# Decoder layer on one core: the q2c part of the last product folded into its weights

## The chip, the cores and the metric

The kernel runs on one core of a Trainium2 chip, in one launch. The metric is the device time in microseconds (us): a median of 748.32 us over three runs (746.5 to 749.77). Engines are named TensorE (PE), VectorE (DVE), ScalarE (ACT), GpSimd (POOL) and SyncE (SP), which issues all DMAs.

## The reference, cut to what matters

The layer has three parts, each added to its input: self-attention on the normalised x (32 x 112 tokens, width 256), a bidirectional attention with a context (32 x 375 tokens), and a mixture of experts. The change lies in the second. With `c` the normalised x (112 x 256) and `q` the context of one batch element:

```
s       = (c @ w_c + b_c)[:, :, None] + (q @ w_q + b_q)[:, None, :] + einsum('bcd,bqd,d->bcq', c, q, w_cq) + b_cq
c2q_att = softmax(s, axis=2) @ q
b_att   = softmax(max(s, axis=2), axis=1)
q2c_att = einsum('bc,bcd->bd', b_att, c)[:, None, :]        # one row of 256 for each batch element
x       = concatenate([c, c2q_att, c * c2q_att, c * q2c_att], axis=-1)
z       = x @ W_l.T + b_l
```

So z is a sum of four products with the four parts W1 to W4 of the 1024 x 256 weights.

## The kernel before, in words

**Stages.** The first stage runs the attention parts over 8 groups of G = 4 batch elements: group 0, a hardware loop over groups 1 to 6, and group 7. It ends at about 433 us of the profile. The second stage, the experts, follows behind a barrier and is the same in both kernels.

**Products.** Products with weights are made in single pass fp32r from operands split in a high and a low part: `mm3` issues three matmuls (lines 75, 76 and 77) for each block of 128 rows. A product of c, c2q or c * c2q with its part of the weights is thus 2 x 3 = 6 matmuls of 112 x 256 for each element, and z takes 24 for each element. Transposes (`turn_...`), the similarity and c2q products are plain fp32.

**Order.** Every engine has its own instruction list, written out by hand in `group(i, last)`, and waits on semaphores. On TensorE a group is: `qk_product`, `scores`, `v_product` (on h), then `z_q2c(i - 1, 0)` and `(i - 1, 1)`, the c * q2c products of the group before; `probs_proj` and `attention_out`; the last two `z_q2c`; then `turn_c`, `z_c`, `similarity`, `turn_a`, `c2q_product` mixed over the four elements; then `turn_x`, `z_c2q`, `z_x3`, with the next group's `turn_h_pair` between them.

**The q2c path.** VectorE ends a group by `x4` = c * q2c (line 1092). ScalarE takes its high part in the next group between the `qk_copy`s (`x4_high`, line 609, named x_hi in the rows), GpSimd its low part (`x4_low`, line 818, x_lo).

**The other paths into a group.** GpSimd: `x4_low(i - 1)`; `residual_bias(i)`, four additions (line 814); the rstd of each element (lines 830 and 832); `ln1_scalars(i + 1)`; and last x2b = x1 + b_l, four additions (line 844), whose first waits for the store of the group before, since they share the x2b buffer. SyncE: the load of x for the group after next (line 320, behind hh and `residual` of the group), the four context pairs, each behind its `c2q_mm` (lines 303 and 304), and then the store of x2 (line 328). All go through one queue. VectorE starts a group by the statistics of the x just loaded (`ln1_stats`, line 863), three of them ahead of the first `score_max` (line 902).

**The c path.** `c_parts(j)` on ScalarE (lines 657 to 661) copies the transposed c, takes its high part, and scales it by w_cq for the similarity; `c_low(j)` on VectorE (line 949) takes the low part. `residual(i + 1)` on ScalarE (line 604) stands ahead of `c2q_copy(0)` (line 674).

Of the kernel before, what the change touches and what calls it, by code (L numbers as in the profile page):

```python
# [30 lines left out]
P = 128  # L31
# [19 lines left out]
def decoder_layer(nc, x, ctx, ctx_t, norm_w, norm_b, qkv_wt, qk_b, v_b, proj_wt, proj_b, w_cq, b_cq, w_c, b_c,  # L51
# [28 lines left out]
    with outer:  # L80
# [102 lines left out]
        with ExitStack() as c1:  # L183
# [50 lines left out]
            x4_hi, x4_lo = sb("x4_hi", [P, G, KB, L], F32R), sb("x4_lo", [P, G, KB, L], F32R)  # L234
# [12 lines left out]
            x4 = ctw  # L247
# [32 lines left out]
            q2c_ok, x4_ok, x4_hi_ok, x4_lo_ok = sem("q2c_ready"), sem("x4_ready"), sem("x4_hi_ready"), sem("x4_lo_ready")  # L280
# [78 lines left out]
            def _(pe):  # L359
# [30 lines left out]
                def z_q2c(g, j):  # L390
                    if j == 0:
                        pe.wait_ge(x4_lo_ok, g + 1)
                    for k in range(KB):
                        last = mm3(pe, z_of(j), x4_hi[:, j, k, :], x4_lo[:, j, k, :], wl_hi[:, 3 * KB + k, :],
                                   wl_lo[:, 3 * KB + k, :], False, k == KB - 1, skip_group_check=True)
                    if j % 2:
                        last.then_inc(z_mm, 1)

                def group(i, last_group):
# [58 lines left out]
                    def z_c(j):  # L458
                        pe.wait_ge(c_lo_ok, ev[j])
                        if j % 2 == 0:  # L460
                            pe.wait_ge(x2_ok, PAIRS * i + j // 2 + 1)
                        if j == 0 and is_first(i):
                            pe.wait_ge(wl_lo_ok, 1)
                        for k in range(KB):
                            mm3(pe, z_of(j), c_hi[:, j, k, :], c_lo[:, j, k, :], wl_hi[:, k, :], wl_lo[:, k, :],
                                k == 0 and j % 2 == 0, False, skip_group_check=True)

                    def similarity(j):
                        pe.wait_ge(cx_in[j], 32 * (i + 1))
                        pe.wait_ge(ctw_ok, ev[j])  # L470
                        pe.wait_ge(c_lo_ok, ev[j])
# [24 lines left out]
                    def z_c2q(j):  # L496
                        pe.wait_ge(x_lo_ok, ev[j])
                        for k in range(KB):
                            t = slice(k * L, (k + 1) * L)
                            mm3(pe, z_of(j), op_hi[j][:, t], op_lo[j][:, t], wl_hi[:, KB + k, :], wl_lo[:, KB + k, :], False, False,  # L500
                                skip_group_check=True)
# [1047 lines left out]
```

## Time and profile before

| what | value |
|---|---|
| runs | 748.32 us median, 746.5 to 749.77 |
| the profiled execution's own time | 747.58 us |
| its span | 745.8 us |
| TensorE matmul busy | 697.2 us (93%), 4072 instructions |
| VectorE, ScalarE, GpSimd busy | 449.7, 358.0, 199.3 us |
| mean granted TensorE clock | 0.983 |
| DMA | 64.43 MB, mean 86 GB/s |

A matmul's busy time includes its pipelined end, so a busy TensorE is not one at its peak: the distance from start to start is what a matmul costs in a row of them. Idle time of an engine counts only where another engine, or the end, waits for what it does next. Where a loop of waits runs over several engines and a transfer, its length is the period of the groups, and the engine with the most busy time need not be the one that sets it.

### The profile page before, as it was taken

The page shows a single profiled execution, that of the slowest core. Times are in us where ns is not written, and L with a number is a line of the kernel's source. Part 1 is how long each engine was busy: PE and PEld are TensorE (multiplying, and loading weights), DVE is VectorE, ACT ScalarE, POOL GpSimd, SP SyncE. Part 2 cuts the span into 40 slices and gives each one's busy share as a digit, 9 for nine tenths or more (in the row PEclk, how much of TensorE's full clock was granted, in tenths as well). Part 3 has the DMA queues.
Part 4 walks back from the last instruction along what each step waited for, and adds up shares of the span by engine and source line. Part 5 has one row for each costly group of instructions (what it writes and reads, how often), then busy time and mean ns, then how long its engine had stood idle before and what let it go on. Part 6 is the DMA issues. An engine that isn't in the chain of part 4 may idle for free. (4 is left out here: it accounts for less than half of the span.)

```text
span 745.8 us, 12056 instructions
## 1 busy us (share of the span) xinstructions
PE 697.2 (93%) x4072; PEld 588.4 (79%) x4072; DVE 449.7 (60%) x1174; ACT 358.0 (48%) x859; POOL 199.3 (27%) x290
## 2 busy tenths in 40 slices
PE   3999999999999999999999866999999999999997
PEld 2867878778788788788787754788888888888886
DVE  5575655755654646557556665766666667666432
ACT  3755663665656556646665323434242333333331
POOL 2142221314204305223141302232223222232222
PEclk9999999999999999999999887999999999999999
DMA  7505024033051060240420266022222212131200
GB/s 210 155 22 165 6 76 141 0 111 103 0 163 51 22 186 6 77 137 0 123 66 1 75 203 218 1 113 85 115 85 113 86 41 107 50 121 50 114 29 29
DMA packets 50765, 64.43 MB, mean 86 GB/s; under 512 B 3800, under 2 KB 49416, under 8 KB 49840
## 3 DMA queue, kind: packets, MB, share of 16 engines
q1 hardware_dynamic: 50736, 64.06, 27.3%
q8 instruction: 16, 0.26, 0.1%
q14 instruction: 13, 0.11, 0.0%
HBM read 56.60 MB, written 7.45 MB: 86 GB/s over the span
## 5 line engine op out<-in xcount | busy, mean ns | idle before, releaser
L1381 POOL TENSOR_TENSOR sg<-sg,cw_wide 128x512 f32<-128x512 f32 x56 | 73.9, 1319 | 186.6 <-ACT sg L1338 177.0
L1342 ACT ACTIVATE a_hi<-af 128x512 fp32r<-128x512 f32 x63 | 39.8, 632 | 155.8 <-DVE af L1462 155.8
L75 PE MATMUL bank<-h_hi,w_lo 128*128 128x512 f32 x224 | 92.4, 412 | 6.5 <-DVE w_lo L1479 4.7
L76 PE MATMUL bank<-h_lo,w_hi 128*128 128x512 f32 x224 | 90.0, 402 | 0.0
L77 PE MATMUL bank<-h_hi,w_hi 128*128 128x512 f32 x224 | 89.6, 400 | 0.0
L1462 DVE TENSOR_TENSOR af<-bank,sg 128x512 f32<-128x512 f32 x63 | 43.2, 686 | 62.0 <-POOL sg L1381 58.9
L1467 DVE TENSOR_TENSOR a_lo<-af,a_hi 128x512 fp32r<-128x512 f32 x63 | 48.1, 763 | 34.9 <-ACT a_hi L1342 34.9
L75 PE MATMUL bank<-w_hi,a_lo 128*128 128x256 f32 x224 | 63.2, 282 | 0.0
L76 PE MATMUL bank<-w_lo,a_hi 128*128 128x256 f32 x224 | 63.2, 282 | 0.0
L77 PE MATMUL bank<-w_hi,a_hi 128*128 128x256 f32 x224 | 63.1, 282 | 0.0
L844 POOL TENSOR_TENSOR x2b<-x,bl_wide 112x256 f32<-112x256 f32 x32 | 23.1, 753 | 146.6 <-DMA x_scratch<-x2b 146.6
L75 PEld LDWEIGHTS bank<-h_hi,w_lo 128*128 128x128 f32 x224 | 43.6, 195 | 17.3 <-DVE w_lo L1479 5.1
L77 PEld LDWEIGHTS bank<-h_hi,w_hi 128*128 128x128 f32 x224 | 43.2, 193 | 10.2
L76 PEld LDWEIGHTS bank<-h_lo,w_hi 128*128 128x128 f32 x224 | 43.6, 195 | 7.9
L486 PE MATMUL bank<-ctxf,at 125*112 125x256 f32 x192 | 46.7, 379 | 0.0
L473 PE MATMUL bank<-ctxtf,ctw 128*112 128x375 f32 x128 | 46.1, 482 | 0.0
L75 PEld LDWEIGHTS bank<-w_hi,a_lo 128*128 128x128 f32 x224 | 42.5, 190 | 2.5 <-DVE a_lo L1467 0.2
L76 PEld LDWEIGHTS bank<-w_lo,a_hi 128*128 128x128 f32 x224 | 42.5, 190 | 2.3
L1338 ACT ACTIVATE sg<-bank 128x512 f32<-128x512 f32 x63 | 37.1, 589 | 12.3 <-PE bank L77 12.1
L77 PEld LDWEIGHTS bank<-w_hi,a_hi 128*128 128x128 f32 x224 | 42.6, 190 | 0.0
L626 ACT ACTIVATE qg<-bank 112x512 f32<-112x512 f32 x32 | 19.1, 598 | 44.7 <-PE bank L410 44.7
L75 PE MATMUL bank<-wp_hi,op_lo 128*128 128x256 f32 x128 | 39.6, 309 | 0.6 <-DVE wp_lo L990 0.6
(226 smaller groups left out, 1901.0 us busy)
## 6 DMA issues: line engine op xcount, KB each, us to landing
cw_wide<-cw_scratch SPq DMA_DIRECT2D x7, 2048.0 KB, 7.1
ctxtf<-in_ctx_t SPq DMA_DIRECT2D x32, 375.0 KB
ctxf<-in_ctx SPq DMA_DIRECT2D x32, 375.0 KB
xt<-in_x SPq DMA_DIRECT2D x8, 448.0 KB, 8.1
x_scratch<-x2b SPq DMA_DIRECT2D x8, 448.0 KB, 10.7
x2n<-x_scratch SPq DMA_DIRECT2D x7, 512.0 KB, 4.8
x2t<-x_scratch SPq DMA_DIRECT2D x7, 512.0 KB, 4.1
out_dram<-x2t SPq DMA_DIRECT2D x7, 512.0 KB, 2.9
```

Of the source, the lines that this page charges most:

```text
L75: pe.matmul(dst, a_lo, b_hi, start=first, stop=False, **kw)
L76: pe.matmul(dst, a_hi, b_lo, start=False, stop=False, **kw)
L77: return pe.matmul(dst, a_hi, b_hi, start=False, stop=last, **kw)
L473: last = pe.matmul(bank[j][0:L, 0:S], ctw[:, j, k, :], ctxtf[:, j, k, :], start=(k == 0), stop=(k == KB - 1))
L486: last = pe.matmul(bank[j][0:L, 0:D], at[:, j, b * L:(b + 1) * L], ctxf[0:SB, j, b, :], start=(b == 0), stop=(b == NSB - 1))
L626: act.activation(qg[j][0:L, :], bank[j][0:L, :], ACT.Copy).then_inc(qk_ok, 1)
L844: pool.tensor_tensor(x2b[:, j, :], x1[:, j, :], bl_wide[:, :], ALU.add).then_inc(x1b_ok, 1)
L1338: act.activation(sg[b][:, :], g_bank[b][:, :], ACT.Silu).then_inc(sg_ok, 1)
L1342: act.activation(a_hi[n % (AHEAD + 1)][:, :], af[(p + n) % 2][:, :], ACT.Copy).then_inc(a_hi_ok, 1)
L1381: pool.tensor_tensor(sg[b][:, :], sg[b][:, :], cw_wide[p][:, ORDER[n], :], ALU.mult).then_inc(sgw_ok, 1)
L1462: dve.tensor_tensor(af[b][:, :], u_bank[b][:, :], sg[b][:, :], ALU.mult).then_inc(af_ok, 1)
L1467: dve.tensor_tensor(a_lo[b][:, :], af[(p + n) % 2][:, :], f32(a_hi[b][:, :]), ALU.subtract).then_inc(a_lo_ok, 1)
```

## The change

The product of c * q2c with W4 equals c times W4 with its rows scaled by q2c. So for each element of a group VectorE now makes wz = W1 + q2c * W4 (`wz_sum`, two instructions of 128 x 256), ScalarE its high part (`wz_high`), GpSimd its low part (`wz_low`), 128 x 512 each, and TensorE one product with c (`z_c`), in the places of `z_q2c` in the next group. The `z_c` between the transposes of c are gone, and `z_c2q` starts the accumulation. w_cq and w_q are applied on VectorE (`c_weighted`). The high part of c is taken once for the group (`c_high`, 128 x 896, on ScalarE), the low part on GpSimd. `residual(i + 1)` moves on ScalarE behind the c2q copies and `x3_high`, ahead of the last `h_high_pair`.

```
-            wl_f = tmp_all[:, :, :].rearrange("p g (k n) -> p (g k) n", n=D)
+            wl_f = sb("wl_f", [P, 4 * KB, D])
-            wl_hi, wl_lo = sb("wl_hi", [P, 4 * KB, D], F32R), sb("wl_lo", [P, 4 * KB, D], F32R)
+            wl_hi, wl_lo = sb("wl_hi", [P, 2 * KB, D], F32R), sb("wl_lo", [P, 2 * KB, D], F32R)
+            wz = sb("wz", [P, G, KB, D])
+            wz_hi, wz_lo = sb("wz_hi", [P, G, KB, D], F32R), sb("wz_lo", [P, G, KB, D], F32R)
...
# TensorE
-                def z_q2c(g, j):
+                def z_c(g, j):
+                    pe.wait_ge(wz_lo_ok, G * g + j + 1)
                     if j == 0:
-                        pe.wait_ge(x4_lo_ok, g + 1)
+                        pe.wait_ge(c_lo_ok, g + 1)
                     for k in range(KB):
-                        last = mm3(pe, z_of(j), x4_hi[:, j, k, :], x4_lo[:, j, k, :], wl_hi[:, 3 * KB + k, :],
-                                   wl_lo[:, 3 * KB + k, :], False, k == KB - 1, skip_group_check=True)
+                        last = mm3(pe, z_of(j), c_hi[:, j, k, :], c_lo[:, j, k, :], wz_hi[:, j, k, :], wz_lo[:, j, k, :],
+                                   False, k == KB - 1, skip_group_check=True)
...
                     attention_out(3)
-                    z_c(0)
                     turn_c(1)
                     similarity(0)
-                    z_c(1)
                     turn_c(2)
...
# ScalarE
+                def wz_high(g, j):
+                    act.wait_ge(wz_ok, G * g + j + 1)
+                    act.activation(wz_hi[:, j, :, :], wz[:, j, :, :], ACT.Copy).then_inc(wz_hi_ok, 1)
...
                     a_columns(2)
+                    c_high()
                     a_columns(3)
-                    if not last:
-                        residual(i + 1)
                     c2q_copy(0)
...
                     x3_high(3)
...
                     else:
+                        residual(i + 1)
                         h_high_pair(i + 1, 1)
# GpSimd
+                def wz_low(g, j):
+                    pool.wait_ge(wz_hi_ok, G * g + j + 1)
+                    pool.tensor_tensor(wz_lo[:, j, :, :], wz[:, j, :, :], f32(wz_hi[:, j, :, :]), ALU.subtract).then_inc(wz_lo_ok, 1)
...
                 def group(i, last):
-                    if not is_first(i):
-                        x4_low(i - 1)
                     residual_bias(i)
+                    if not is_first(i):
+                        for j in range(G):
+                            wz_low(i - 1, j)
...
                         ln1_scalars(i + 1)
+                    pool.wait_ge(c_hi_ok, i + 1)
+                    pool.tensor_tensor(c_lo[:, :, :, :], ct[:, :, :, :], f32(c_hi[:, :, :, :]), ALU.subtract).then_inc(c_lo_ok, 1)
# VectorE
+                    def c_weighted(j):
+                        dve.wait_ge(ct_ok, ev[j])
+                        for k in range(KB):
+                            w = dve.tensor_scalar(ctw[:, j, k, :], ct[:, j, k, :], wcq[:, k:k + 1], wq[:, k:k + 1], ALU.mult, ALU.add)
+                        w.then_inc(ctw_ok, 1)
+                    def wz_sum(j):
+                        for k in range(KB):
+                            w = dve.scalar_tensor_tensor(wz[:, j, k, :], wl_f[:, 3 * KB + k, :], q2c[:, j, k:k + 1], wl_f[:, k, :], ALU.mult, ALU.add)
+                        w.then_inc(wz_ok, 1)
```

On GpSimd, from the last step of `ln1_scalars` in the loop over groups to the first rstd of the group behind it, before (x2b is x1 with its bias, x4_lo the low part of c * q2c, x2n the residual with its bias, r2a and r2 the rstd):

```order
L809 TENSOR_TENSOR ln1<-ln1,mone 112x4 [waits ln1_scalars]
L843 REGISTER_ALU [waits c_ready]
L844 TENSOR_TENSOR x2b<-x1,bl_wide 112x256 [waits x2_stored]
L844 TENSOR_TENSOR x2b<-x1,bl_wide 112x256 [waits c_ready] x3
L852 REGISTER_ALU
L852 COMPARE_AND_BRANCH
L818 TENSOR_TENSOR x4_lo<-ctw,x4_hi 128x896 [waits x4_hi_ready]
L814 TENSOR_TENSOR x2n<-x2n,pb_wide 112x256 [waits residual_scaled] x4
L830 TENSOR_TENSOR r2a<-mv2,eps 112x1 [waits ln2_moments]
L832 TENSOR_TENSOR r2<-r2a,mhalf 112x1 [waits ln2_var_eps]
```

and in the changed kernel:

```order
L795 TENSOR_TENSOR ln1<-ln1,mone 112x4 [waits ln1_scalars]
L826 TENSOR_TENSOR c_lo<-ct,c_hi 128x896 [waits c_hi_ready]
L832 REGISTER_ALU [waits c_ready]
L833 TENSOR_TENSOR x2b<-x1,bl_wide 112x256 [waits x2_stored]
L833 TENSOR_TENSOR x2b<-x1,bl_wide 112x256 [waits c_ready] x3
L842 REGISTER_ALU
L842 COMPARE_AND_BRANCH
L800 TENSOR_TENSOR x2n<-x2n,pb_wide 112x256 [waits residual_scaled] x4
L804 TENSOR_TENSOR wz_lo<-wz,wz_hi 128x512 [waits c_weights_hi] x4
L817 TENSOR_TENSOR r2a<-mv2,eps 112x1 [waits ln2_moments]
L819 TENSOR_TENSOR r2<-r2a,mhalf 112x1 [waits ln2_var_eps]
```

The low part stood ahead of the four residual additions as one instruction; now it stands behind them as four, one for each element. The low part of c is new, ahead of the x2b additions and their wait for the store.

On TensorE, from the last attention product of a group to the second similarity, before (bank4 holds z of elements 0 and 1; c_lo with wl_hi is the c product):

```order
L449 MATMUL bank3<-qg3,v 112x256
L461 ISA [waits c_lo_ready]
L75 MATMUL bank4<-wl_hi,c_lo 112x256 [waits x2_ready]
L76 MATMUL bank4<-wl_lo,c_hi 112x256
L77 MATMUL bank4<-wl_hi,c_hi 112x256
L75 MATMUL bank4<-wl_hi,c_lo 112x256
L76 MATMUL bank4<-wl_lo,c_hi 112x256
L77 MATMUL bank4<-wl_hi,c_hi 112x256
L455 MATMUL bank1<-ident,c 128x112 [waits c_ready]
L455 MATMUL bank1<-ident,c 128x112
L469 REGISTER_ALU
L473 MATMUL bank0<-ctxtf,ctw 112x375 [waits c_lo_ready,c_weighted,context0_in]
```

and in the changed kernel:

```order
L451 MATMUL bank3<-qg3,v 112x256
L457 MATMUL bank1<-ident,c 128x112 [waits c_ready]
L457 MATMUL bank1<-ident,c 128x112
L464 MATMUL bank0<-ctxtf,ctw 112x375 [waits c_weighted,context0_in]
L464 MATMUL bank0<-ctxtf,ctw 112x375
L457 MATMUL bank2<-ident,c 128x112 [waits c_ready]
L457 MATMUL bank2<-ident,c 128x112
L464 MATMUL bank1<-ctxtf,ctw 112x375 [waits c_weighted,context1_in]
```

The six matmuls for each element that stood among transposes and similarities are gone, and with them the waits for the low part of c; the q2c product, now c with wz, stays where it was.

On ScalarE, behind the copies of the attention columns (at) of a group, before (x2n is the residual, tmp the copied c2q):

```order
L686 ACTIVATE at<-bank2 125x336 [waits a_transposed]
L686 ACTIVATE at<-bank3 125x336 [waits a_transposed]
L604 ACTIVATE x2n<-xt,ln1 112x256 [waits x1_ready,ln1_scalars,x_in]
L674 ACTIVATE tmp<-bank0,sinv2 112x256 [waits sim_inv_sum,c2q_product]
L674 ACTIVATE tmp<-bank1,sinv2 112x256 [waits sim_inv_sum,c2q_product]
L678 ACTIVATE op_hi0<-bank0 128x224 [waits c2q_transposed]
```

and in the changed kernel, at the end of the group:

```order
L665 ACTIVATE op_hi3<-bank3 128x224 [waits c2q_transposed]
L669 ACTIVATE op_hi2<-tmp 128x224 [waits c_c2q_ready]
L669 ACTIVATE op_hi3<-tmp 128x224 [waits c_c2q_ready]
L595 ACTIVATE x2n<-xt,ln1 112x256 [waits x1_ready,ln1_scalars,x_in]
L609 ACTIVATE h3_hi0<-bank7 128x2x224 [waits h_transposed]
```

The residual stood ahead of the c2q copies; now it stands behind the last high part of c * c2q and ahead of the last high part of h.

## Rows read from the trace of the kernel before

**Rows 1.** The longest waits: engine, line, releaser: us in total, times, longest.
```profile
POOL x2b L844 <- DMA x_scratch<-x2b: 146.6, 7, 22.9
...
DVE st L863 <- DMA xt<-in_x: 38.2, 7, 6.9
```

**Rows 2.** SyncE's queue in order of time: start, us, engine, line, transfer issued.
```profile
156.12 0.39 SPq L303 DMA_DIRECT2D ctxtf<-in_ctx_t  x1
...
167.10 3.08 SPq L328 DMA_DIRECT2D x_scratch<-x2b  x1
...
170.88 0.70 SPq L320 DMA_DIRECT2D xt<-in_x  x1
...
206.94 0.39 SPq L303 DMA_DIRECT2D ctxtf<-in_ctx_t  x1
```

**Rows 3.** GpSimd in order of time, at the turn from one group to the next.
```profile
177.84 2.81 POOL L844 TENSOR_TENSOR x2b<-x,bl_wide 112x256 f32<-112x256 f32 x4 [21.74 <-DMA x_scratch<-x2b]
...
180.61 2.09 POOL L818 TENSOR_TENSOR x_lo<-ctw,x_hi 128x896 fp32r<-128x896 f32 x1
...
182.66 2.82 POOL L814 TENSOR_TENSOR x2n<-x2n,pb_wide 112x256 f32<-112x256 f32 x4
```

**Rows 4.** VectorE in order of time, the same stretch.
```profile
179.05 1.08 DVE L863 BATCH_NORM_STATS2 st<-xt 112x6 f32<-112x256 f32 x3 [5.70 <-DMA xt<-in_x]
...
180.04 0.68 DVE L902 TENSOR_REDUCE smx<-bank 128x2 f32<-128x512 f32 x1
```

**Rows 5.** TensorE in order of time: the q2c product and the projection products behind it.
```profile
131.95 0.37 PE L75 MATMUL bank<-wl_hi,x_lo 128*112 128x256 f32 x1 [0.82 <-POOL x_lo L818]
...
182.96 0.28 PE L75 MATMUL bank<-wl_hi,x_lo 128*112 128x256 f32 x1
...
184.25 0.28 PE L77 MATMUL bank<-wl_hi,x_hi 128*112 128x256 f32 x1
...
184.40 0.39 PE L75 MATMUL bank<-wp_hi,op_lo 128*128 128x256 f32 x1
...
189.24 1.02 PE L449 MATMUL bank<-qg,v 128*112 128x256 f32 x4
```

**Rows 6.** TensorE in order of time: from the c product to the c2q product.
```profile
144.91 0.37 PE L75 MATMUL bank<-wl_hi,c_lo 128*112 128x256 f32 x1
...
154.49 1.46 PE L486 MATMUL bank<-ctxf,at 125*112 125x256 f32 x6
...
160.74 0.41 PE L493 MATMUL bank<-ident,tmp 112*128 112x112 f32 x2 [1.47 <-ACT tmp L674]
```

**Rows 7.** VectorE in order of time: the fourth element's normalised rows.
```profile
148.99 0.41 DVE L930 TENSOR_SCALAR c<-x,mv,r 112x256 f32<-112x256 f32 x1 [0.36 <-POOL r L832]
```

**Rows 8.** TensorE in order of time: what follows its four longest gaps after the start.
```profile
419.21 0.57 PE L493 MATMUL bank<-ident,tmp 112*128 112x112 f32 x2 [3.21 <-DVE mrow L1069]
...
442.52 0.80 PE L75 MATMUL bank<-h_hi,w_lo 128*128 128x512 f32 x1 [4.72 <-DVE w_lo L1479]
...
451.63 1.73 PE L130 MATMUL bank<-ident,h 128*128 128x128 f32 x7 [3.75 <-DVE h L163]
...
463.02 0.41 PE L174 MATMUL bank<-h_lo,gate 128*16 128x512 f32 x1 [3.69 <-DVE h_lo L169]
```

**Rows 9.** Stretches of 1 us: stretch, length, busy time of each engine, PEclk, DMA share, GB/s.
```profile
426.00:427.00 1.00, 1.00 (x10) 1.00 (x9) 1.00 (x4) 0.95 (x1) 0.00 (x0) 0.92 0.00 0
...
446.00:447.00 1.00, 1.00 (x4) 0.76 (x4) 0.96 (x4) 0.00 (x0) 0.00 (x0) 0.68 0.87 261
...
456.00:457.00 1.00, 1.00 (x4) 0.81 (x3) 0.00 (x0) 0.00 (x0) 0.00 (x0) 0.56 0.89 377
...
463.00:464.00 1.00, 0.98 (x4) 0.55 (x5) 1.00 (x2) 0.66 (x1) 1.00 (x1) 0.85 0.00 0
...
467.00:468.00 1.00, 1.00 (x5) 0.79 (x5) 1.00 (x2) 1.00 (x3) 0.18 (x1) 0.94 0.00 0
```

**Rows 10.** One VectorE line: times in ns (min, median, max), first and last start.
```profile
L163 DVE TENSOR_SCALAR h<-x2n,mv,r x28: 399/409/1506, 425.9 to 666.1; 128x256 f32<-128x256 f32 x28
```

More of the change, by code:

```diff
@@ L456, in turn_c @@
                         last.then_inc(t_c, 1)
[L458 to L466, printed above, removed]
                     def similarity(j):
@@ L546, in group @@
                     similarity(2)
-                    z_c(2)
                     turn_a(0)
@@ L550, in group @@
                     turn_a(1)
-                    z_c(3)
                     c2q_product(0)
@@ L696, in group @@
                     if not is_first(i):
-                        x4_high(i - 1)
+                        wz_high(i - 1, 0)
                     qk_copy(2)
                     if not is_first(i):
+                        wz_high(i - 1, 1)
                         v_copy(0)
+                        wz_high(i - 1, 2)
                     qk_copy(3)
+                    if not is_first(i):
+                        wz_high(i - 1, 3)
                     if is_first(i):
@@ L763, in group @@
                     if last:
-                        x4_high(i)
+                        for j in range(G):
+                            wz_high(i, j)
                         h3_high(act, 0, h3_hi0)
@@ L826, in group @@
                     residual_bias(i)
+                    if not is_first(i):
+                        for j in range(G):
+                            wz_low(i - 1, j)
                     def rstd2(j):
@@ L846, in group @@
                         rstd3(pool, 0)
-                        x4_low(i)
+                        for j in range(G):
+                            wz_low(i, j)
                 pool.wait_ge(consts, 4)
@@ L1019, in group @@
                     dve.wait_ge(st2_ok, ev[2])
-                    c_low(0)
+                    c_weighted(0)
                     x1_moments(2)
@@ L1024, in group @@
                     c_rows(2)
-                    c_low(1)
+                    c_weighted(1)
                     dve.wait_ge(st2_ok, ev[3])
@@ L1028, in group @@
                     x1_moments(3)
-                    if is_first(i):
-                        wl_low(3)
-                    else:
+                    if not is_first(i):
                         x2_sum(i - 1, 1)
                     c_rows(3)
-                    c_low(2)
+                    c_weighted(2)
                     sim_max(1)
-                    c_low(3)
+                    c_weighted(3)
                     if is_first(i):
@@ L1085, in group @@
                     for k in range(KB):
-                        w = dve.tensor_tensor(x4[:, :, k, :], ct[:, :, k, :], b_wide, ALU.mult)
+                        w = dve.tensor_tensor(cb[:, :, k, :], ct[:, :, k, :], b_wide, ALU.mult)
                     w.then_inc(cb_ok, 1)
                     dve.wait_ge(cb_ok, i + 1)
-                    dve.reduce_sum(q2c[:, :, :], x4[:, :, :, :], AX).then_inc(q2c_ok, 1)
+                    dve.reduce_sum(q2c[:, :, :], cb[:, :, :, :], AX).then_inc(q2c_ok, 1)
                     dve.wait_ge(q2c_ok, i + 1)
-                    for k in range(KB):
-                        w = dve.tensor_tensor(x4[:, :, k, :], ct[:, :, k, :], q2c[:, :, k].unsqueeze(2).to_broadcast([P, G, L]), ALU.mult)
-                    w.then_inc(x4_ok, 1)
+                    for j in range(G):
+                        wz_sum(j)
                     if last:
```

71 lines of the change are left out of this document (26 added, 45 removed).

## The prediction

> **What bounds the kernel now.** The page's busy times put TensorE first, but they are means over two stages, and only the first stage changes. So I read the waits first. GpSimd waits 146.6 us in 7 places for the store of x2, and VectorE 38.2 us in 7 for the load of x [rows 1]; both come once for each group from group 1 or 2 on, so a transfer lies in the path of the groups. Then the queue of SyncE: a group's first context load is issued at 156.12, the next group's at 206.94, a period of 50.82 us. Behind the first load stand three more pairs, then the store of x2 (167.10), then x (170.88) [rows 2]. The first load is released by the first c2q product, which starts at 154.49 and has 1.46 us of busy time [rows 6]. The store has landed at 177.84, where GpSimd starts x2b [rows 3]: this leg is 177.84 - 156.12 = 21.72 us. x has landed at 179.05 [rows 4].
>
> From the landing of the store, called L, a chain runs: x2b, x4_lo at L + 2.77, done at L + 4.86 [rows 3], and the q2c product on TensorE. In one group TensorE waited 0.82 us for it [rows 5]; in the group shown the product starts at 182.96, L + 5.12, just behind it. A twin chain runs over x: three statistics, `score_max` at 180.04, and the softmax, whose last part (op_lo) lets the projection start at 184.40, L + 6.56, two hundredths behind the twelfth q2c matmul [rows 4, 5]. From that projection (one period earlier 133.58) to the first context load take 22.54 us. The loop closes: 6.56 + 22.54 + 21.72 = 50.82. TensorE's work and this loop thus end almost together; a TensorE matmul saved counts only if it lies in the loop, and work added in the loop counts in full.
>
> **The change part by part.**
>
> *Matmuls.* 24 fewer for each group. The pitch is (184.25 - 182.96) / 11 = 0.117 us [rows 5], so 2.8 us for each group, 22.5 us over eight. All 24 stand between the projection and the first c2q product, in the loop. But c now goes through transpose, copy, `c_weighted` and similarity with less beside it. Followed along the lists: the first similarity starts 0.8 us earlier, the second 1.4; then the fourth element's normalised rows wait for GpSimd's rstd, as before at 148.99 with 0.36 us [rows 7], and now TensorE waits some 0.6 us there, and 0.2 us in two smaller places. The first c2q product, before at 154.49 [rows 6], comes at about 152.27: 2.2 us saved of 2.8. Before, the projections took 189.24 - 184.40 = 4.84 us for 36 matmuls [rows 5], paced by the softmax; at 0.117 they take 4.2. With the softmax done ahead of them, as below, this gives 0.57 more. Together 2.8 us; bounds 2.2 (all waits doubled) and 3.4 (no wait).
>
> *GpSimd.* It loses x4_lo (2.09) from the loop's head and gets `residual_bias` ahead of four wz_low. The trace has no 128 x 512 with an fp32r output. Bounds: x2n's 0.70 for 256 columns and x_lo's 2.09 for 896 [rows 3]; on the line between them 512 columns take 1.26. So wz_low(0) ends at L + 2.77 + 2.82 + 1.26 = L + 6.85 and wz_low(1) at L + 8.11. The second `z_c` waits for the latter, and the projection stands behind it: 8.11 + 0.03 + 6 x 0.117 = L + 8.85. Before it was L + 6.56, so 2.3 us are lost. This takes the place of the wait for x: the softmax, ready at L + 6.56, is covered. Low parts three and four end at L + 10.6, ahead of their products.
>
> *The period.* 8.85 + (22.54 - 2.8) + 21.72 = 50.3 us, 0.5 less than before. The leg of 21.72 is unchanged, since the transfers behind the first context load are issued one on the other [rows 2]; 0.5 either way.
>
> *Other edits.* c_weighted (two instructions) for c_low on VectorE, and c_high and ctw off ScalarE: in the c chain above. c_high (0.95 by x4_high's size) stands in a pause of ScalarE; c_lo (2.1) ends before GpSimd's wait for the store. wz_sum and wz_high: VectorE and ScalarE wait there for x and for TensorE. The residual ahead of c2q_copy made TensorE wait 1.47 us at 160.74 [rows 6]; that wait goes, and with it about 0.2 more, 1.66 in all. It lies behind the release of the context load, outside the loop: TensorE comes earlier to `z_c` and waits there. The x load, now behind the later residual, is still behind the store in SyncE's queue, so it loses nothing.
>
> *The gap.* Before, TensorE took 182.96 - 154.49 = 28.47 us from the first c2q product to the q2c product [rows 5, 6]. Now it needs 26.8 and wz_low(0) comes at 1.63 + 21.72 + 6.85 = 30.2. So in each of groups 2 to 7 TensorE stands for about 3.4 us ahead of `z_c(0)`, less the 0.17 by which a matmul's busy time outlasts its pitch: 3.2. Gaps of this size are rare in the trace and each had a price: behind gaps of 3.21, 4.72, 3.75 and 3.69 us [rows 8] the granted clock was at half, 1.2 GHz, until 426.2, 446.6, 456.9 and 467.1 (read from the share of the last 1 us stretch [rows 9]), that is for 7.0, 4.1, 5.2 and, as it was still full until 463.7, 3.4 us of work. Behind 1.47 us it stayed at 2.4 GHz. Half clock for H us loses H / 2, but the first 1.28 of it are hidden by the wait for wz_low(1). Loss: 2.8, 1.4, 2.0 and 1.1 us; mean 1.8. I take 1.2, the mean of the two where fp32r products followed the gap at once, as here; in the two others transposes and a product of four rows came first [rows 8]. Bounds 0 and 2.8.
>
> The Trainium skill (TensorE: Matmul & The Clock Gate, Part 1) says that the throttled clock is the default, and that only activity releases it. It speaks against this change, which saves matmuls in order to wait; by it each gap is paid, as in rows 8 and 9, and the sum is the one below with its loss; without it, it would be 7 us less.
>
> *Ends.* Group 0 has neither store nor q2c product; its first c2q product comes 2.2 earlier, and so does x for group 1. Group 1 has no store to wait for (its buffer is free from the start), stays on the x chain, and saves 2.2 once more: 4.4 us up to its context load. Groups 2 to 7 give 0.5 each: 3.0, less 0.2 for group 7, whose softmax has no x to wait for. The tail pays: wz_sum takes 2.8 us where x4 took 1.2, its four high and low parts stand ahead of the last products: 0.2 us net, since TensorE is busy with z_x3 until then. Sum without the clock: -4.4 - 2.8 + 0.2 = -7.0. With the clock: + 6 x 1.2 = +7.2. Net +0.2 on the profiled execution's 747.58, which lies 0.74 under the median of 748.32: forecast 748.5 us, no change.
>
> A rule that would add to it: the Trainium skill (GPSIMD Engine Reference, Specifications) says GpSimd shares its SBUF interfaces with VectorE when that runs in a two-port mode or reads two SBUF inputs. The trace agrees: one VectorE tensor_scalar line takes 399 to 1506 ns [rows 10]. Here it would hold `normalise_h` back behind c_lo by up to 2.1 us, which falls into the gap above and shortens it. The sum stays, and the clock's fall becomes a little less certain.
>
> **The rivals.**
> A, no fall of the clock: the gaps stay under what costs it. For it: 3.2 us is the shortest gap that cost anything, and the shared interface may shorten it. Against: four of four fell. Time: 748.3 - 7.0 = 741.3 us.
> B, the slower side: each gap costs what the first one cost, 2.8 us, as 3.21 us is the gap nearest in length [rows 8, 9]. Place: from `z_c(0)` over the projections, six times. Time: 748.3 - 7.0 + 16.8 = 758 us. It is slower than before from 1.2 us a group on, and measurably from 1.8.
> C, the loop isn't one: the store or x lands early enough, because the transfers follow TensorE. Then the matmuls and the wait of 1.47 are all gained: 2.8 + 1.6 for seven groups, 31 us, 717 us. Against: the loop's three terms meet the period to the hundredth. Half of it, with a leg shortened by 2 us, would be about 733.
> D, GpSimd's new work isn't in the way (wz_low much shorter than the line): x binds instead, the projection is at L + 6.56, period 50.82 - 2.2 = 48.6, 15 us in all, 733 us. Against: x_lo took 2.09 in the same place.
>
> **How the numbers follow.** Forecast 50%, own range 744 to 753 (loss 0.6 to 1.9 a group); A 17%; B 23%; C and D together 10%. For 8 in 10 the range takes in A and goes most of the way to B: 740 to 756. A measurement tells 0.5%, 3.7 us, from no change: faster is under 744.6, slower over 752.1. The forecast gives 0.05, 0.37 and 0.08; A, C and D 0.27 faster, of which 0.02 may fall to same; B 0.23, of which 0.03 may. Faster 0.28, same 0.44, slower 0.28.
>
> **What would show it.** GpSimd: wz_low(0) directly behind the residual additions, at 1.26 us each, and TensorE's longest total wait for it, about 3 us for each of six groups, where before 0.8 was seen once. PEclk under 1.0 for 3 to 7 us behind each. The wait for tmp (1.47) gone. First context load to x2b 21.7 us, as before. A period near 51.5 us. Wrong if TensorE doesn't wait for wz_lo (C or D), if the clock stays at 1.0 (A), or if the period exceeds 53 (B).

## The result, and the profile after

The changed kernel takes 762.54 us (median of 4 runs, 758.81 to 764.54), the kernel before 748.19 us (4 runs) beside it: a ratio of 1.019, 95% interval 1.017 to 1.021. It is slower. The forecast was 748.5 us, no change, in a range of 740 to 756. The profiled execution took 758.81 us, the quickest of the four, with a span of 756.8 us against 745.8: 11.0 us more. These 11 us can be placed in the two traces. The median's other 3 us are the spread between executions; the three longer ones also had a lower mean granted clock, 0.956 to 0.963 against 0.966. No trace places these 3 us.

First the page of the changed kernel: busy time, share of the span and count of instructions for each engine.

```profile
PE 686.8 (91%) x3880; PEld 577.7 (76%) x3880; DVE 482.9 (64%) x1252; ACT 346.7 (46%) x793; POOL 240.3 (32%) x322
```

TensorE does 192 matmuls less, GpSimd is busy for 41 us more. The next fence holds its waits (engine, line, releaser: us in total, times, longest):

```profile
POOL x2b L833 <- DMA x_scratch<-x2b: 113.5, 7, 19.2
...
PE bank L75 <- POOL wz_lo L804: 19.9, 6, 4.1
...
PE bank L130 <- DVE h L163: 9.7, 3, 6.0
```

GpSimd still waits for the store of x2 seven times, as in [rows 1]. Where TensorE once waited 0.82 us for x_lo [rows 5], it now waits six times for wz_lo. The turn from one group to the next, in order of time, SyncE's queue first, then GpSimd, which answers to [rows 2, 3]:

```profile
258.20 0.39 SPq L304 DMA_DIRECT2D ctxtf<-in_ctx_t  x1
...
269.09 3.43 SPq L329 DMA_DIRECT2D x_scratch<-x2b  x1
```
```profile
280.06 2.79 POOL L833 TENSOR_TENSOR x2b<-x,bl_wide 112x256 f32<-112x256 f32 x4 [18.23 <-DMA x_scratch<-x2b]
282.82 2.77 POOL L800 TENSOR_TENSOR x2n<-x2n,pb_wide 112x256 f32<-112x256 f32 x4
285.55 4.98 POOL L804 TENSOR_TENSOR wz_lo<-wz,wz_hi 128x512 fp32r<-128x512 f32 x4
```

And TensorE there, with the stretches of 1 us in which it resumes (columns as in [rows 9]):

```profile
286.86 0.56 PE L75 MATMUL bank<-wz_hi,c_lo 128*112 128x256 f32 x1 [3.15 <-POOL wz_lo L804]
```
```profile
286.00:287.00 1.00, 0.14 (x1) 0.14 (x1) 1.00 (x3) 1.00 (x5) 1.00 (x2) 0.50 0.00 0
287.00:288.00 1.00, 1.00 (x5) 1.00 (x6) 0.90 (x4) 1.00 (x4) 1.00 (x1) 0.50 0.00 0
291.00:292.00 1.00, 1.00 (x7) 1.00 (x6) 0.00 (x0) 0.00 (x0) 0.00 (x0) 0.50 0.00 0
292.00:293.00 1.00, 1.00 (x8) 1.00 (x8) 0.00 (x0) 0.64 (x2) 0.00 (x0) 0.66 0.00 0
```

These rows show the forecast loop: first context load 258.20, landing 280.06, `z_c(0)` at 286.86, that is 6.80 us behind the landing; then the column PEclk at 0.50, 1.2 GHz, for 5.8 us. In the other five groups the half clock lasted until 2.8 to 5.2 us behind the start of `z_c(0)`.

Where the 11.0 us lie, by the issue of two loads of SyncE: group 1's first context load (before 104.13, changed 100.83) and the load of the norm in the last group (411.65 and 416.23).

| stretch | before | changed | difference | forecast |
|---|---|---|---|---|
| start to group 1's first context load | 104.1 | 100.8 | -3.3 | -4.4 |
| six periods up to the norm's load | 307.5 | 315.4 | +7.9 | +4.4 |
| from there to the end | 334.2 | 340.6 | +6.4 | +0.2 |

The last line holds the surprise. In the changed kernel's last group (VectorE, GpSimd and TensorE in order of time):

```profile
428.88 6.29 DVE L945 SCALAR_TENSOR_TENSOR wz<-wl_f,q2c 128x256 f32<-128x256 f32 x8
...
430.50 4.39 POOL L804 TENSOR_TENSOR wz_lo<-wz,wz_hi 128x512 fp32r<-128x512 f32 x3 [3.93 <-ACT wz_hi L600]
...
435.09 2.32 DVE L163 TENSOR_SCALAR h<-x2n,mv,r 128x256 f32<-128x256 f32 x4
...
437.47 1.97 PE L130 MATMUL bank<-ident,h 128*128 128x128 f32 x8 [6.05 <-DVE h L163]
```

and before:

```profile
424.81 1.16 DVE L1092 TENSOR_TENSOR ctw<-ct,q2c 128x448 f32<-128x448 f32 x2
425.88 1.38 DVE L163 TENSOR_SCALAR h<-x2n,mv,r 128x256 f32<-128x256 f32 x4
...
428.75 1.03 PE L130 MATMUL bank<-ident,h 128*128 128x128 f32 x8
```

From the start of the sums to that of h took 6.2 us, where x4 took 1.1; h itself 2.32 instead of 1.38; and TensorE, idle for 6.05 us, came back at half clock.

The longer time isn't spread over the eight sums. Here are all eight (ns: min, median, max), and the last of them with the wz_low beside it:

```profile
L945 DVE SCALAR_TENSOR_TENSOR wz<-wl_f,q2c x8: 478/484/1500, 428.9 to 433.7; 128x256 f32<-128x256 f32 x8
```
```profile
433.45 1.44 POOL L804 TENSOR_TENSOR wz_lo<-wz,wz_hi 128x512 fp32r<-128x512 f32 x1
433.69 1.48 DVE L945 SCALAR_TENSOR_TENSOR wz<-wl_f,q2c 128x256 f32<-128x256 f32 x1
```

Five sums took 0.48 us. The three that started while a wz_low was under way took 1.48 to 1.50 and ended 0.28 us behind its end. So did the fourth h (1.35 us for 0.40, ending 0.15 us behind). What such a meeting cost was the rest of GpSimd's instruction.

### The profile page after: what moved, and what is told of

Its sections match the earlier page's. It is cut to its first block and busy times, and to the rows that moved or that the text cites. A ratio compares the mean times of both kernels' runs of the same rounds, so it can differ in the third digit from the quotient of the medians.

```text
span 756.8 us, 11792 instructions
## 1 busy us (share of the span) xinstructions
PE 686.8 (91%) x3880; PEld 577.7 (76%) x3880; DVE 482.9 (64%) x1252; ACT 346.7 (46%) x793; POOL 240.3 (32%) x322
## 5 line engine op out<-in xcount | busy, mean ns | idle before, releaser
L902 DVE SCALAR_TENSOR_TENSOR op_lo<-bank,sinv,op_hi 128x256 fp32r<-128x256 f32 x64 | 28.0, 480 | 36.3 <-ACT op_hi L631 35.6
L477 PE MATMUL bank<-ctxf,at 125*112 125x256 f32 x192 | 46.7, 379 | 0.0
L804 POOL TENSOR_TENSOR wz_lo<-wz,wz_hi 128x512 fp32r<-128x512 f32 x32 | 40.8, 1303 | 10.7 <-ACT wz_hi L600 10.7
L75 PE MATMUL bank<-wz_hi,c_lo 128*112 128x256 f32 x64 | 24.7, 385 | 19.9 <-POOL wz_lo L804 19.9
## 6 DMA issues: line engine op xcount, KB each, us to landing
x_scratch<-x2b SPq DMA_DIRECT2D x8, 448.0 KB, 10.8
```

What stands on the lines that cost most here:

```text
L75: pe.matmul(dst, a_lo, b_hi, start=first, stop=False, **kw)
L477: last = pe.matmul(bank[j][0:L, 0:D], at[:, j, b * L:(b + 1) * L], ctxf[0:SB, j, b, :], start=(b == 0), stop=(b == NSB - 1))
L804: pool.tensor_tensor(wz_lo[:, j, :, :], wz[:, j, :, :], f32(wz_hi[:, j, :, :]), ALU.subtract).then_inc(wz_lo_ok, 1)
L902: w = dve.scalar_tensor_tensor(op_lo[j][:, n], bank[j][:, n], sinv[:, j, half:half + 1], f32(op_hi[j][:, n]), ALU.mult, ALU.subtract)
```

## The experiments

"The period" of a kernel is the mean of the last four stretches between the first context loads of two groups: 51.0 us before, 52.2 in the changed kernel. "Changed" is the kernel of the result above. All ratios are to the kernel before, in runs on the same chip.

**1. GpSimd's wz_low ahead of the residual additions.**
```diff
-                    residual_bias(i)
                     if not is_first(i):
                         for j in range(G):
                             wz_low(i - 1, j)
+                    residual_bias(i)
```


> The changed kernel, with GpSimd's four wz_low of the last group ahead of the four residual additions instead of behind them. Loop theory: the period of groups 2 to 7 runs from the landing of the x2 store over GpSimd's x2b and its wz_low to TensorE's z_c, and every microsecond there counts. The first wz_low then ends 2.77 us (x2b) + 1.28 us = 4.1 us after the landing instead of 6.83, the gap ahead of z_c(0) falls from 3.2 us to about 0.5, the clock no longer falls behind it (1.4 us a group), so 4 us a group, six groups: 762.5 - 24 = 738 us. Rival, VectorE theory: the groups are longer because VectorE has taken over the weighting of c and the sums (33 us more busy time), not because of GpSimd's queue: within 2 us of 762. Between them, if only the wait goes and the clock falls all the same: 746. The tail behind the last group (+6.4 us) stays in all of them.

Measured 742.5 us, ratio 0.993 (0.991 to 0.995): 20 us from the changed kernel by putting two steps in the other order. The waits ahead of `z_c(0)` were 0.2 to 0.9 us in five of six groups and the clock stayed at 1.0 there; in the first of the six the wait was 1.92 us and the clock fell behind it. The period was 49.2 us, 3.0 less and not 4: the first attention_out starts 11.4 us behind the landing, which is 6.56 + 4.84, the softmax of the kernel before [rows 4, 5]. TensorE now waits 0.25 to 0.29 us for the softmax's low part (op_lo, line 902) in four groups, so the twin chain over x seems to have taken over. For these 20 us it was GpSimd's order that counted, and not VectorE's extra work; experiment 11 shows what a part of that work cost.

**2. In the last group GpSimd waits until all high parts are there.**
```diff
                     if last:
                         rstd3(pool, 0)
+                        pool.wait_ge(wz_hi_ok, G * (i + 1))
```


> The changed kernel, with one more wait: in the last group GpSimd starts its four wz_low only when all four high parts are there, and so VectorE's eight wz_sum instructions run with GpSimd idle. Sharing theory: the 6.29 us of the last group's sums against eight of 0.48 us (3.84) come from GpSimd reading and writing SBUF at the same time; they fall to 3.84, the h of the norm behind them from 2.32 us to 1.4, and turn_h3 starts 3.4 us sooner. The last wz_low ends about 0.9 us later than now, which z_c(3) takes back in part: total 1 to 3 us less, 760.5. Rival: the sums are slow for a reason of their own (first use of their operands behind the reduction): they stay at 6.3 us, and the total rises by the 1 to 4 us by which the lows come later: 765.

Measured 756.69 us, 1.012 (1.010 to 1.014); the stretch behind the norm's load took 336.5 us, 4.1 less. An added wait made the kernel faster, by more than I expected. VectorE and GpSimd in the last group:

```profile
430.23 3.26 DVE L946 SCALAR_TENSOR_TENSOR wz<-wl_f,q2c 128x256 f32<-128x256 f32 x8
433.40 2.47 DVE L163 TENSOR_SCALAR h<-x2n,mv,r 128x256 f32<-128x256 f32 x4
434.23 5.25 POOL L804 TENSOR_TENSOR wz_lo<-wz,wz_hi 128x512 fp32r<-128x512 f32 x4 [6.30 <-ACT wz_hi L600]
```

The same eight sums take 3.26 us alone and 6.29 beside wz_low. The h behind them stays long: its fourth instruction now meets a wz_low and takes 1.50 us.

**3. The gap filled.** v_product(1), not otherwise changed, is computed three times over in all groups but the first, so TensorE works where it waited.
```diff
-                        for k in range(KB):
-                            last = mm3(pe, v_bank[half][:, 0:TOK], ...)
+                        for _ in range(3 if half == 1 and not is_first(i) else 1):
+                            for k in range(KB):
+                                last = mm3(pe, v_bank[half][:, 0:TOK], ...)
```


> The changed kernel, in which TensorE makes v_product(1) of groups 1 to 7 three times over (same result, 2.4 us more of matmuls) where it now idles 3.2 us ahead of z_c(0). The wait's end is not touched. Clock theory: the granted clock stays at 2.4 GHz behind the gap, and z_c(0) to the first attention_out shrinks from 7.6 us (mean of six) to the 6.3 us that all-fast matmuls make: 1.4 us a group, 762.5 - 8 = 754 us, and no half clock in the 1-us windows behind z_c(0). Rival: the half clock there is off the path, since VectorE or ScalarE sets the first attention_out: same time within 1.5 us though the clock is up. Third: a group is a chain with slack, and the added 2.4 us of matmuls cost: slower, 765 and more.

Measured 756.83 us, 1.012 (1.010 to 1.014). In groups 3 to 7 the waits were 0.2 to 1.2 us, the clock stayed at 1.0, and the period was 51.1 us instead of 52.2: the clock's price is 1.1 us a group. (In group 2 a wait of 1.90 us was left, and the clock fell behind it.) In the group without a store to wait for the repeats cost 3.9 us (53.57 for 49.63), which is why the sum is 5.7 us between the medians (2.4 between the spans) and not 8. With 12 matmuls a group more the kernel is faster.

**4. The loop cut: the store of x2 ahead of the context loads.**
```diff
+                    if not is_first(i):
+                        sp.wait_ge(x2_ok, PAIRS * (i + 1))
+                        sp.dma_start(x2_tiles[...], x2b[:, :, :]).then_inc(x2_st, 16)
                         for j in range(G):
                             sp.wait_ge(c2q_mm, G * i + j + 1)
                             load_context(batch + G, j)
-                    if not is_first(i):
-                        sp.wait_ge(x2_ok, PAIRS * (i + 1))
-                        sp.dma_start(x2_tiles[...], x2b[:, :, :]).then_inc(x2_st, 16)
```


> The changed kernel, with the store of x2 of the group before put ahead of the four context loads in SyncE's queue instead of behind them (its own wait, x2_ok, is over some 15 us before the first context load may start). Loop theory: this cuts the loop. x2b no longer waits for the landing, GpSimd has its wz_low done before TensorE asks, the gap of 3.3 us and the half clock behind it (1.4 us) go in all groups from 2 on: a period of about 47.8 us instead of 52.5, 762.5 - 28 = 734 us. Rival: something else ends just behind (the x load and its statistics on VectorE, or GpSimd's one queue, in which x2b now stands behind c_lo): the period stays near 51 and the time above 752.

Measured 736.35 us, 0.986 (0.982 to 0.990), period 48.6. No wait for wz_lo is left. TensorE's waits from 101 to 350 us show what ends next:

```profile
PE bank L75 <- DVE op_lo L925: 6.1, 5, 1.2
PE bank L465 <- DVE ctw L941: 1.8, 10, 0.2
PE bank L458 <- DVE c L921: 1.5, 5, 0.3
```

**5. The residual back ahead of the c2q copies.**
```diff
                     a_columns(3)
+                    if not last:
+                        residual(i + 1)
                     c2q_copy(0)
@@
                     else:
-                        residual(i + 1)
                         h_high_pair(i + 1, 1)
```


> The changed kernel, with ScalarE's residual(i+1) back ahead of the four c2q copies. In the kernel before it cost TensorE a wait of 1.47 us at turn_x in each group. Loop theory: in the changed kernel groups 2 to 7 are set by the chain store landing, x2b, residual additions, wz_low, z_c, ..., context loads, store; the leg from the first context load to the landing took 21.7 us with the wait (before) and 21.4 to 22.0 without it (changed), because the context loads' own transfers fill it. So the wait comes back and is hidden; group 1, which no loop holds, and the first group may lose 1.5 us each, while the x load may start earlier: 762.5, between 760 and 765. Rival: a wait of TensorE always costs, 1.47 us in 7 groups: 772.

Measured 755.3 us, 1.011 (1.008 to 1.014). Both accounts missed: giving TensorE its wait back made the kernel 7 us faster (3.6 us between the two spans). TensorE's waits from 101 to 415 us:

```profile
PE bank L75 <- POOL wz_lo L805: 12.7, 11, 2.9
PE bank L484 <- ACT tmp L661: 8.8, 6, 1.5
```

`z_c(0)` is still 6.84 us behind the landing. TensorE comes 1.47 us later to it and waits 1.2 to 1.95 us in five of the six groups, and the clock stays at 1.0 behind these; behind the one of 2.86 us it was at half. From `z_c(0)` to the first attention_out takes 6.35 us instead of 7.6. The period is 51.0, against which the first two groups lose 1.5 us each, as expected. Here one wait of 3.2 us costs 1.3 us more than the same time in two pieces.

**6. The same early store in the kernel before.** The diff is that of 4.

> The kernel before, with the store of x2 ahead of the four context loads in SyncE's queue, as in e4_store_early. That edit took 26 us from the changed kernel. TensorE theory: from 156 to 360 us of the kernel before TensorE is busy for 198.1 of 204 us at the full clock and waits only for the residual's place in ScalarE's queue (1.47 us, four times); the chain through the store exists there but has slack. Then nothing changes: 748, within 2 us. Rival, the loop as I forecast it: the period of 50.8 us was already set by the store's landing, and cutting it frees at least 3 us in each of six groups: 730 or less. Third: the store's transfer now lies beside the context loads and delays them: up to 752.

Measured 744.71 us, 0.995 (0.994 to 0.997). Three microseconds: the loop I had read was there, but TensorE's own work, with the residual's wait in it, ended only 0.44 us a group ahead of it on average. The period went from 51.0 to 50.6, and the only wait of any size is still the residual's, 1.47 us six times.

**7. Last group: norm first, low parts on VectorE.**
```diff
+                    if last:
+                        normalise3(dve, 0)
                     for j in range(G):
                         wz_sum(j)
                     if last:
-                        normalise3(dve, 0)
+                        for j in range(G):
+                            dve.wait_ge(wz_hi_ok, G * i + j + 1)
+                            dve.tensor_tensor(wz_lo[:, j, :, :], wz[:, j, :, :], f32(wz_hi[:, j, :, :]), ALU.subtract).then_inc(wz_lo_ok, 1)
```
(and the four wz_low off GpSimd there)

> The changed kernel, in which the last group's norm (normalise3) stands ahead of the sums wz_sum on VectorE, and the last group's four wz_low run on VectorE behind them instead of on GpSimd beside them. All other groups are as they were. Sharing theory: h starts at once behind q2c (1.4 us) and turn_h3 about 7 us sooner than in the changed kernel, the sums take 3.3 us as they did when GpSimd idled, the lows 4 x 0.6 = 2.4 us, the last z_c can start 7.1 us behind q2c. The last x2 store goes out some 10 us behind q2c instead of 15.8. The time from the norm's load to the end falls from 340.6 by 5 to 6.5 us: 757. Rival: the tail is long because z_c of the last group runs at half the clock behind any gap: the gain stays at the 3.9 us that the added wait gave, 758.5 or more.

Measured 756.44 us, 1.012 (1.009 to 1.015); the stretch behind the norm's load is 336.0 us, 4.6 less. VectorE:

```profile
431.84 1.38 DVE L163 TENSOR_SCALAR h<-x2n,mv,r 128x256 f32<-128x256 f32 x4
433.13 3.25 DVE L943 SCALAR_TENSOR_TENSOR wz<-wl_f,q2c 128x256 f32<-128x256 f32 x8
...
436.30 2.49 DVE L1090 TENSOR_TENSOR wz_lo<-wz,wz_hi 128x512 fp32r<-128x512 f32 x4
```

All three at the length expected with GpSimd idle. Of the tail's 6.4 us, 4.6 went with the sharing and the order; 1.8 are left with the work itself, not taken apart. The clock still falls there, from 438.3 to 441.7 us.

**8. Experiment 4, with GpSimd's c_lo and x2b behind VectorE's normalise_h.**
```diff
+                    if not last:
+                        pool.wait_ge(hh_ok, G * (i + 2))
                     pool.wait_ge(c_hi_ok, i + 1)
```


> e4_store_early with one more wait: GpSimd starts its c_lo and x2b of a group only when VectorE has normalised the next group's rows (hh). In e4 the four normalise_h took 3.92 us together beside c_lo and x2b against 1.36 in the kernel before, and TensorE waited 1.21 us for op_lo behind them in each group. Sharing theory: they fall to 1.4 us, the wait goes, and the period falls from 48.5 to about 47.3 us: 736.4 - 7 = 729 us. Rival: normalise_h is slow for the load of x beside it or its place in the queue, and GpSimd starting later makes x2b and the lows late: 736 or more.

Measured 734.02 us, 0.982 (0.980 to 0.984). The same VectorE line in 4 and in 8 (ns: min, median, max):

```profile
L867 DVE TENSOR_SCALAR h<-xt,mv,ln x32: 407/824/2148, 11.1 to 349.6; 112x256 f32<-112x256 f32 x32
```
```profile
L869 DVE TENSOR_SCALAR h<-xt,mv,ln x32: 393/397/415, 10.9 to 345.8; 112x256 f32<-112x256 f32 x32
```

The median halves, and TensorE's wait behind it is gone. Only 2.3 us came of it, not 7, as another took its place: up to 1.3 us for probs_low (op_lo, line 905), which stands behind the statistics that wait for x. That this order is the cause is what experiment 10 tests.

**9 and 10. Experiments 7 and 8 together (9), and the statistics of the next x behind probs_low (10).**
```diff
-                    if not last and not is_first(i):
-                        ln1_stats(i + 1, 0)
...
                     score_max(0)
-                    if not last and not is_first(i):
-                        ln1_stats(i + 1, 3)
                     score_max(1)
...
                     probs_low(3)
+                    if not last and not is_first(i):
+                        for j in range(G):
+                            ln1_stats(i + 1, j)
```


> e8_store_early_apart and e7_tail_on_vector together: store early, c_lo and x2b behind the normalised rows, and the last group's norm and lows on VectorE. The loop and the tail are different places, so the two gains should add: 734.0 less the 4.6 us that e7 took from the time behind the norm's load: 729.5 us. Rival: the tail's gain is bound to the old kernel's state there: 732 or more.

> e9_all, with the four statistics of the next group's x behind the four probs_low on VectorE instead of ahead of and between the first score maxima. In e8 they wait 4.07 us there for the x load, which now leaves behind the residual, and TensorE waits 0.75 us for probs_low in some groups. If that wait is the load's doing, 0.75 us a group go: 3 to 4 us less than e9_all, 726 us. Rival: the statistics then stand in the way of x1_sum, and the same time is lost at the attention output: 729.5 or more.

Measured 728.76 us (0.973, 0.971 to 0.975) and 721.55 us (0.965, 0.963 to 0.967): the tail's gain adds, and the late statistics give 7.2 us where 3 to 4 were expected. The wait for probs_low was not the whole of it: the period fell by 1.1 us to 47.3.

**11. The weighting of c back on ScalarE in the changed kernel.**
```diff
                         act.activation(ct[:, j, :, :], ...).then_inc(ct_ok, 1)
+                        act.wait_ge(ct_ok, ev[j])
+                        for k in range(KB):
+                            w = act.activation(ctw[:, j, k, :], ct[:, j, k, :], ACT.Identity, bias=wq[:, k:k + 1], scale=wcq[:, k:k + 1])
+                        w.then_inc(ctw_ok, 1)
```
(and the four c_weighted off VectorE, with one small copy in the place of the first)

> The changed kernel, with the weighting of c back on ScalarE (two instructions of 0.48 us a batch behind each c copy, where VectorE takes 0.33). It undoes that part alone. Loop theory: the c part of the changed kernel waits 0.67 us a group for VectorE (0.31 for c, twice 0.18 for the weighted c). ScalarE's two take 0.96 instead of 0.66 behind the copy and delay the next copy, so TensorE waits some 0.3 to 1 us more at each similarity, on the leg from z_c to the first context load, which is in the loop: 1 to 3 us a group slower, 768 to 780. Rival, that the weighting's move to VectorE was what cost: faster than 760.

Measured 754.25 us, 1.009 (1.006 to 1.011): the rival's side. ScalarE's two instructions are longer but stand directly behind their copy, while VectorE's stood between its other work. From the first attention_out to the context load takes 15.3 us instead of 15.87, the waits for the weighted c are gone, the period is 51.4. The spans differ by 4.7 us, the medians by 8. So this part of VectorE's extra work did cost.

**12. Experiment 10 with the weighting on ScalarE, the best version.**

> e10_all_stats_late with the weighting of c on ScalarE, as in e11, which gave 8 us in the changed kernel. In e10 TensorE still waits 0.31 us for c and twice 0.18 us for the weighted c in each group. If these waits are what the weighting on VectorE costs, 0.65 us a group go, 717 us. Rival: e11's gain came from the loop's leg and, the loop being cut here, nothing is left of it: 721.5.

Measured 716.66 us, 0.959 (0.957 to 0.960), as expected: 4.9 us from 10, period 46.7.

**13. The kernel before with the early store, the late residual and the late statistics.**

> The kernel before with those edits of e10 that apply to it: the x2 store ahead of the context loads, the residual behind the c2q copies, the four statistics behind probs_low. It still makes the separate products of c and of c times q2c with their weights, 24 matmuls a group more than the changed kernel, 2.9 us at 0.12 us each. TensorE theory: with every wait gone the two kernels differ by that work: a period near 49.5 us against 47.3, 735 to 738 us against e10's 721.6. Rival: the kernel before can't use these edits (e6 gave it 3 us) and stays at 744.

Measured 730.7 us, 0.977 (0.975 to 0.979), better than expected. TensorE from 101 to 345 us, first here, then in experiment 12:

```profile
101.00:345.00 244.00, 244.00 (x1515) 208.81 (x1514) 152.42 (x446) 149.33 (x416) 72.27 (x140) 1.00 0.28 82
```
```profile
101.00:345.00 244.00, 239.60 (x1464) 203.06 (x1463) 164.49 (x479) 164.04 (x433) 110.46 (x164) 1.00 0.31 90
```

The first never stands still; its period of 48.5 us is its matmuls. The second has 24 matmuls a group less and 0.8 us of waits, and its period is 46.7. With the loop cut on both sides the change is worth 14 us (730.7 to 716.7), of the 22.5 that its matmuls amount to. It is then the change without its move of the weighting to VectorE, and with the repairs of experiments 7 and 8 to its own side effects.

**14. The loop kept, with the edits of 5, 7 and 11.**

> The changed kernel with the store where it was, so the loop is kept, but the residual ahead of the c2q copies (e5, 7 us less), the weighting on ScalarE (e11, 8 us less) and the last group's norm and lows on VectorE (e7, 6 us less). Sum theory: the three act in different places and add: 741 us, a period near 50 us in groups 2 to 7. Rival: e5 and e11 both only kept the clock up behind the gap at z_c(0), and don't add: 749.

Measured 746.74 us, 0.998 (0.996 to 1.000), between the two. In the profiled execution groups in which the clock held have a period of 50.4 us, as the sum says; in four of six it fell again, behind waits of 2.63, 1.64, 2.50 and 1.38 us, and these took 51.8 to 53.5 (the last up to the norm's load). Waits of 1.69 and 1.75 us were free. So the gains add where the clock holds, but it fell behind 1.38 and 1.64 us and held behind 1.69 and 1.75: the length of such a wait alone doesn't tell. Its ten runs spread over 7.4 us (742.8 to 750.3), where the five of experiment 12 spread over 2.1.

## Why the prediction was wrong, point by point

- **Landing to z_c, right.** L + 6.85 was forecast, 6.80 to 6.83 measured in all six groups; wz_low on the line between two sizes, 1.26, measured 1.28. TensorE's wait of 3.2 us came as 3.3 on average (19.9 / 6).
- **The clock, right in kind, a little small.** Half clock behind each of the six gaps. From `z_c(0)` to the first attention_out took 7.07 to 8.38 us, mean 7.63, against 6.35 with the clock up (experiment 5): 1.3 us a group for the 1.2 taken; the filled gap gave 1.1. By the Trainium skill (TensorE: Matmul & The Clock Gate, Part 1) the throttled clock is the default, and activity releases it. Experiment 3, which fills the wait with matmuls and leaves its end alone, agrees: the granted clock is 1.0 in groups 3 to 7, where it was 0.5 behind each gap. Rival B (2.8 us each) is out, though its time of 758 came nearest; rival A is out.
- **The residual outside the loop: right, but priced at nothing.** The saved 1.47 us did turn into waiting at `z_c`. I gave this edit no price, but it is what made a gap of 1.2 to 1.95 us, which cost nothing in five groups of experiment 5, into one of 3.2 that the clock pays for. The loss stood in the sum, under the gap; it belonged to this edit, at +1.3 us a group.
- **"2.2 us saved of 2.8", too large.** From the first attention_out to the context load the saving was 17.70 - 15.87 = 1.83 us; forecast were 2.2 us. The weighting's place on VectorE takes it: back on ScalarE in experiment 11 it gives 0.53 us, and the saving is 2.4.
- **"The leg of 21.72 is unchanged", right, though the number was one group's.** From the first context load to the landing it took 21.96 us on average of the six groups before and 22.01 in the changed kernel. One period was likewise taken for all: the six before are 51.25 us on average, and not 50.82. Compared average with average, the 3.5 us by which the six periods missed (+7.9 for +4.4) are placed: 2.2 from the first attention_out to the context load (1.83 us saved for 2.2), 1.0 from the landing to the first attention_out (3.09 us lost for 2.92), 0.3 the leg.
- **"Ends: 4.4" came as 3.3.** In group 0 TensorE waited 1.17 us for op_lo and 1.09 for h, both behind normalise_h, whose four instructions took 4.36 us there beside c_lo and x2b; the kernel before has neither wait. Its row in the changed kernel and GpSimd's are

```profile
54.25 2.08 POOL L826 TENSOR_TENSOR c_lo<-ct,c_hi 128x896 fp32r<-128x896 f32 x1
54.33 4.36 DVE L866 TENSOR_SCALAR h<-xt,mv,ln 112x256 f32<-112x256 f32 x4 [0.83 <-POOL ln L795]
...
56.28 3.00 POOL L833 TENSOR_TENSOR x2b<-x,bl_wide 112x256 f32<-112x256 f32 x4
```

  I had named that mechanism and put its cost into the later gap; group 0 has no such gap.
- **The tail, the failed step.** "wz_sum takes 2.8 us where x4 took 1.2 ... 0.2 us net" was 6.4: the largest part of the miss, 6.2 us of the 10.8 between the two spans (the periods missed by 3.5, the ends by 1.1). The sums take 3.26 us alone (a little off) and 6.29 beside GpSimd's low parts, h grew by 0.9, and `z_c` came behind the 6 us gap at half clock. The reason given for 0.2, that TensorE is busy with z_x3 until then, did not hold: TensorE waited 6.05 us for h. I applied the rule of the Trainium skill (GPSIMD Engine Reference, Specifications), shared SBUF interfaces, to normalise_h and not to wz_sum, which reads two SBUF inputs in the one place where nothing hides it. Experiments 2, 7 and 8 agree with the rule: with GpSimd kept away the sums take 3.26 and 3.25 us together instead of 6.29, and normalise_h never more than 0.42 us instead of up to 2.15. Keeping them apart and putting h first took 4.6 of the tail's 6.4 us back (experiment 7).
- **The loop in the kernel before.** It closed to the hundredth, but that didn't show how firmly it bound: every chain that ends in one period closes. TensorE's work ended within 0.5 us of it (experiment 6). Rival C's large gains need both limits moved: cut loop alone 3 us, with the waits of TensorE cleared 17 (experiment 13), with the product removed too 31 (experiment 12). That is its 717 us, but by edits that the change didn't have.
- **The chances were added up wrongly.** The terms as given make 0.30 for faster and 0.42 for same, where I wrote 0.28 and 0.44; slower stays at 0.28.

## What to carry to other kernels

Work saved on the busiest engine pays only if the chain that releases it is shortened as well; ask for each wait that goes where TensorE will stand instead, and whether two short waits become one that the clock notices. Removing a wait made this kernel slower, and adding one made it faster. When work moves to an engine that stood idle, look at what its neighbour on the same memory does at that moment, above all in the last group, where nothing hides it. And try the order of the DMA queue first: one store put ahead of four loads took 26 us off the changed kernel, more than the 14 that the change is worth at its best, though only 3 off the kernel before, where TensorE's own work was nearly as long as the loop.

## What the runs showed of the hardware that was not expected

- Waits of TensorE ahead of `z_c(0)`, an fp32r product, six groups each in eight kernels: the twenty-four of 2.66 to 4.57 us in the changed kernel and experiments 2, 7 and 11 were all followed by half clock, which lasted until 2.8 to 6.2 us behind the wait; so were those of 2.50, 2.63 and 2.86 us in 5 and 14. Of the twelve of 1.24 to 1.95 us in 1, 3, 5 and 14, four were (1.38, 1.64, 1.90 and 1.92 us) and eight were not. The nine below 1.2 us in 1 and 3 were not.
- VectorE beside GpSimd: a scalar_tensor_tensor of two SBUF inputs took 0.48 us alone and 1.48 to 1.50 when a wz_low was under way at its start, and ended 0.28 us behind that wz_low; a tensor_scalar from SBUF to SBUF took 0.40 us and up to 2.15, and ended 0.15 us behind c_lo, x2b or wz_low. GpSimd's wz_low took 1.28 us (median) and 1.35 to 1.58 in these meetings.
